# Rows of all batches as one stream of 14 tiles behind the attention, with a ring of three buffers for lifted products

## The reference

```python
def ffn(x, W1, b1, W2, b2):              # _quantize(W) = clip(round(W / (mean|W| + EPS)), -1, 1)
    h = relu(einsum('bsd,fd->bsf', x, _quantize(W1)) + b1)
    return einsum('bsf,df->bsd', h, _quantize(W2)) + b2
# xattn: layer norms with gains of both inputs, then softmax(q k^T * 32**-0.5) v, then @ Wo + bo
x = x + tanh(g_xattn[0]) * xattn(layernorm(x), ctx_1024, ...)
x = x + tanh(g_ffn[0]) * ffn(layernorm(x), ...)
```

## Time and profile before

| what | us |
|---|---|
| median of three runs | 971.6 (966.1 to 974.96) |
| the profiled execution, its own time | 969.31 |
| its span in the trace | 967.4 |
| PE busy | 902.7 (93%) |
| DVE busy | 734.4 (76%) |
| ACT busy | 644.1 (67%) |
| POOL busy | 303.1 (31%) |

### The profile page before, as it was taken

The page is one execution under the profiler, slowest core; times in us unless marked ns, Lnnn a source line. Parts: engine busy times, 40 slices in busy tenths (PEclk is TensorE's granted clock), DMA queues, the critical chain, the costliest instruction groups (busy, mean ns, idle before and its releaser), DMA issues.

```text
span 967.4 us, 22558 instructions
## 1 busy us (share of the span) xinstructions
PE 902.7 (93%) x8996; PEld 694.0 (72%) x8996; DVE 734.4 (76%) x1376; ACT 644.1 (67%) x1330; POOL 303.1 (31%) x519
## 2 busy tenths in 40 slices
PE   2998898899999999999999999999999999889768
PEld 0555566666798688867888688967887688668747
...
GB/s 270 139 228 222 180 110 195 165 135 1 8 138 153 24 2 92 101 127 1 32 113 175 2 2 105 109 106 1 43 102 90 2 2 144 62 29 2 24 19 20
DMA packets 52104, 84.02 MB, mean 87 GB/s; under 512 B 6520, under 2 KB 33592, under 8 KB 51000
## 3 DMA queue, kind: packets, MB, share of 16 engines
...
q10 hardware_dynamic: 432, 0.02, 0.0%
...
## 4 chain that ended last, share of the span: by engine, by line
PE 78%; DVE 9%; DMA 5%; SPq 3%; ACT 3%; issue 1%; POOL 1%; DVEq 0%; ACTq 0%; POOLq 0%
PE ps_fill L477 49%; PE ps_pv L524 8%; PE ps_score L492 7%; PE ps_exp L508 7%; PE ps_fill L534 4%; DMA ctx_raw<-ctx_in 2%; DVE row_max L785 2%; SPq L398 2%; DVE p_parts L793 2%; PE ps_fill L583 2%; DMA h_parts<-w2t 2%; DMA k_stack<-k_stage_lo 1%; SPq L407 1%; DVE ctx_t_lo L870 1%; DVE bn L825 1%
## 5 line engine op out<-in xcount | busy, mean ns | idle before, releaser
L793 DVE TENSOR_TENSOR p_parts<-ps_exp,p_parts 125x448 f16<-125x448 f32 x384 | 231.4, 617 | 61.5 <-ACT ps_exp L664 59.5
L785 DVE TENSOR_REDUCE row_max<-ps_score 128x1 f32<-128x750 f32 x256 | 238.7, 933 | 47.4 <-PE ps_score L492 46.6
L663 ACT ACTIVATE p_parts<-ps_exp 125x448 f16<-125x448 f32 x384 | 209.1, 544 | 94.6 <-PE ps_exp L508 81.0
L664 ACT ACTIVATE ps_exp<-ps_exp 125x448 f32<-125x448 f32 x384 | 211.2, 550 | 0.0
L492 PE MATMUL ps_score<-k_stack,q_stack 96*128 96x375 f16 x512 | 126.7, 329 | 13.2 <-DVE row_max L785 12.2
L508 PE MATMUL ps_exp<-q_stack,k_stack 99*125 99x224 f16 x768 | 128.0, 266 | 9.3 <-DVE p_parts L793 6.3
L524 PE MATMUL ps_pv<-v_now,p_parts 125*128 125x66 f16 x3072 | 115.3, 194 | 2.4 <-DVE p_parts L793 1.9
L477 PE MATMUL ps_fill<-w_ternary,h_parts 128*128 128x256 fp8e4 x1024 | 116.6, 273 | 0.0
L524 PEld LDWEIGHTS ps_pv<-v_now,p_parts 125*128 125x128 f16 x3072 | 110.0, 98 | 8.3 <-DVE p_parts L793 2.1
L508 PEld LDWEIGHTS ps_exp<-q_stack,k_stack 99*125 99x125 f16 x768 | 88.0, 138 | 33.8 <-DVE p_parts L793 9.3
L477 PEld LDWEIGHTS ps_fill<-w_ternary,h_parts 128*128 128x128 f16 x1024 | 99.7, 98 | 13.2 <-DVE ctx_t_lo L870 1.2
...
## 6 DMA issues: line engine op xcount, KB each, us to landing
...
```

The costliest lines, as they stand in the source:

```text
L663: nc.scalar.activation(ph[0:KR, unit, :], ps_exp[0:KR, u, 0:2 * NQ], ACT.Exp, scale=EXP_SCALE)
L664: nc.scalar.activation(ps_exp[0:KR, u, 0:2 * NQ], ps_exp[0:KR, u, 0:2 * NQ], ACT.Exp, scale=EXP_SCALE).then_inc(exp_done, 1)
L785: nc.vector.tensor_reduce(mx[:, i // 2, i % 2:i % 2 + 1], ps_score[:, :, 0:KH], AX.XY, ALU.max) \
L793: nc.vector.tensor_tensor(pl[0:KR, unit, :], ps_exp[0:KR, u, 0:2 * NQ], ph[0:KR, unit, :], ALU.subtract).then_inc(p_split, 1)
```

## The change

Four things are changed together.

1. **A stream of 14 tiles.** Behind the attention the 8 x 224 rows are one stream of 1792 rows. Batch n handles the tiles that are complete with it: 1, 2, 2, 2, 1, 2, 2, 2 for n = 0 to 7. `o_t` holds two halves of 256 columns, and `ot` may write a piece in each. `op`, `norm2`, `yt`, `f2`, `store` follow `tiles_of(n)`; `f1` streams 256 columns in a batch of two tiles and 128 in a batch of one.
2. **`mr` in two matmuls.** The maxima of a pair of heads are 4 stationary columns, and ACT writes the four rows into both heads; a mask in four rows of `k_stack` (`minus_m`, made with `pick`) takes the right two. The shift is added to the maxima by `split`.
3. **A ring of three.** `lifted` has three buffers for `q`, `k` and `f1` in place of two and two. A lift waits until POOL has made the low part of the lift three before it (`parted`).
4. **Another order.** OPENING, ROUND and ENDING are written anew. Small tiles are put into memory that is free at the time, and constants are set in another way.

```diff
+TILES = B * NQ // P
-SPLIT_ROWS = 3 * HD
-MAX_END = SPLIT_ROWS + 2
-STACK_ROWS = MAX_END + 1
+STACK_ROWS = SPLIT_ROWS + 4
...
+def tiles_before(n):
+    return n * NQ // P
+def tiles_of(n):
+    return tiles_before(n + 1) - tiles_before(n)
+LIFTS = [s for s in STEPS if s[0] in ("q", "k", "f1")]
+LIFT_AT = {s: k for k, s in enumerate(LIFTS)}
...
-        qk_full = sb("qk_full", [P, 2, 2 * NQ], F32)
-        h_full = sb("h_full", [P, 2, 2 * NQ], F32)
-        o_t = [sb(f"o_t_{part}", [P, DC, NQ], F16) for part in ("hi", "lo")]
+        lifted = sb("lifted", [P, 3, 4 * P], F32)
+        o_t = [sb(f"o_t_{part}", [P, 2, DC, 2 * P], F16) for part in ("hi", "lo")]
...
+        PARTED = {"q": (qk_split, 10, 0), "k": (qk_split, 10, 2), "f1": (h_split, 8, 0)}
+        def parted(kind, i, n):
+            s, per_batch, first = PARTED[kind]
+            return s, n * per_batch + (first + i + 1)
+        def o_pieces(t, n):
+            at, end = n * NQ - tiles_before(n) * P, tiles_before(n + 1) * P - n * NQ
+            frm, to = q_cols(t)
+            cut = min(max(end, to.start), to.stop)
+            found = [(to.start, cut, n % 2, at), (cut, to.stop, (n + 1) % 2, -end)]
+            return [(slice(a - QSTART[t], b - QSTART[t]), half, slice(a + add, b + add))
+                    for a, b, half, add in found if b > a]
...
                 elif kind == "mr":
                     pe.wait_ge(max_split, n * 8 + (i + 1))
-                    for h in (2 * i, 2 * i + 1):
-                        for t in range(2):
-                            frm, to = q_cols(t)
-                            last = pe.matmul(
-                                ps_fill[SPLIT_ROWS:MAX_END, bank, (h % 2) * NQ + to.start:(h % 2) * NQ + to.stop],
-                                mhl[:, h, t, :], ident16[:, frm], start=True, stop=True,
-                                tile_position=(0, SPLIT_ROWS))
+                    for t in range(2):
+                        frm, to = q_cols(t)
+                        last = pe.matmul(ps_fill[SPLIT_ROWS:STACK_ROWS, bank, to], mhl[:, t, 2 * i:2 * i + 2, :],
+                                         ident16[:, frm], start=True, stop=True, tile_position=(0, SPLIT_ROWS))
...
                 elif kind == "f1":
+                    wide = tiles_of(n) * P
                     for j in range(2):
                         m = slice((2 * i + j) * P, (2 * i + j + 1) * P)
-                        last = three(ps_fill[:, bank, j * NQ:(j + 1) * NQ], lambda a, c: w1q[:, c, m],
-                                     lambda a, c: o_t[a][:, c, :], order=((0, 0), (0, 1)))
+                        last = three(ps_fill[:, bank, j * wide:(j + 1) * wide], lambda a, c: w1q[:, c, m],
+                                     lambda a, c: o_t[a][:, n % 2, c, 0:wide], order=((0, 0), (0, 1)))
...
                 act.wait_ge(fill_ready, ready)
+                if kind in ("q", "k", "f1"):
+                    lift = LIFT_AT[kind, i, n]
+                    if lift >= 3:
+                        act.wait_ge(*parted(*LIFTS[lift - 3]))
```

More of the change, by code:

```diff
@@ L65 @@
[L65 to L79, removed]
@@ L100 @@
-    part.14@1 part.15@1 max.20@1 pv.5@1 stat.6@3 expo.20@1 yt.1@0 part.16@1 expo.21@1 max.21@1 k.7@2 stat.7@3
-    score.23@1 f1.0@0 norm.6@3 part.17@1 score.24@1 take.4@1 part.18@1 f1.1@0 expo.22@1 score.25@1 f1.2@0 yt_lo.0@0
-    expo.23@1 score.26@1 v.3@2 pv.6@1 v_lo.2@2 take.5@1 expo.24@1 expo.25@1 max.22@1 vc.2@1 part.19@1 rstd.0@3
-    yt_lo.1@0 part.20@1 score.27@1 norm.0@3 max.23@1 v.4@2 score.28@1 max.24@1 expo.26@1 mr.5@1 pv.7@1 k_hi.6@2
-    expo.27@1 f1.3@0 f1.4@0 split.5@1 f1_hi.0@0 max.25@1 max.26@1 pv.8@1 expo.28@1 reload.13@0 mr.6@1 part.21@1
@@ new lines @@
+    ternary.13@0 score.12@1 part.3@1 max.10@1 yt_lo.1@0 expo.8@1 part.4@1 ot_lo.0@0 max.11@1 k.3@2 part.5@1
+    split.2@1 take.0@1 max.12@1 k_hi.1@2 part.6@1 ot_lo.1@0 pv.1@1 score.13@1 expo.9@1 op.0@0 expo.10@1 mr.2@1
+    score.14@1 k.4@2 score.15@1 v.0@2 expo.11@1 expo.12@1 pv.2@1 part.7@1 expo.13@1 part.8@1 max.13@1 ternary.14@0
+    stat.0@3 op_add.0@0 max.14@1 k_hi.2@2 rstd2.0@0 score.16@1 stat.1@3 stat.2@3 v.1@2 score.17@1 mr.3@1 reload.10@0
+    kq.2@1 expo.14@1 vc.1@1 reload.11@0 reload.12@0 kq.3@1 norm2.0@0 max.15@1 pv.3@1 part.9@1 expo.15@1 split.3@1
@@ new lines @@
+    f1.1@0 score.25@1 k.7@2 norm.1@3 expo.25@1 norm.2@3 max.19@1 norm.3@3 score.26@1 v.4@2 score.27@1 norm.6@3
+    f1.2@0 max.20@1 v_lo.2@2 k_hi.5@2 pv.7@1 expo.26@1 stat.7@3 rstd.0@3 score.28@1 part.18@1 mr.5@1 f1.3@0
+    expo.27@1 score.29@1 max.21@1 f1.4@0 k_hi.6@2 max.22@1 take.5@1 part.19@1 part.20@1 part.21@1 max.23@1 expo.28@1
+    pv.8@1 mr.6@1 v_lo.3@2 max.24@1 expo.29@1 score.30@1 norm.4@3 max.25@1 expo.30@1 part.22@1 f1_hi.0@0 max.26@1
+    v.5@2 f1_hi.1@0 part.23@1 split.5@1 k_hi.7@2 split.6@1 take.6@1 part.24@1 max.27@1 cx.0@3 v_lo.4@2 part.25@1
@@ L131 @@
-    f1.0@-1 part.17@0 norm.0@2 score.24@0 stat.6@2 rstd.0@2 mr.4@0 part.18@0 expo.22@0 pv.6@0 expo.23@0 f1.1@-1
-    score.25@0 max.21@0 take.4@0 expo.24@0 yt_lo.0@-1 f1.2@-1 part.19@0 expo.25@0 f1.3@-1 pv.7@0 v_lo.2@1 stat.7@2
-    mr.5@0 score.26@0 expo.26@0 max.22@0 norm.1@2 f1.4@-1 ctx.0@2 yt_lo.1@-1 score.27@0 norm.6@2 max.23@0 part.20@0
-    v.3@1 store.0@-2 k_hi.6@1 expo.27@0 take.5@0 expo.28@0 max.24@0 part.21@0 expo.29@0 norm.2@2 v.4@1 score.28@0
-    expo.30@0 pv.8@0 f1.5@-1 part.22@0 vc.3@0 v.5@1 f1_hi.0@-1 expo.31@0 score.29@0 expo.32@0 f1_hi.1@-1 split.5@0
@@ L170 @@
-    op.1@7 yt.0@7 yt.1@7 f1.0@7 ot_lo.1@7 op_add.0@7 bias.0@7 f1.1@7 f1.2@7 f1.3@7 op_add.1@7 f1.4@7 rstd2.0@7
-    yt_lo.0@7 yt_lo.1@7 xb.0@7 f1_hi.0@7 f1.5@7 f1_hi.1@7 f1_hi.2@7 store.0@7 f1.6@7 f1_hi.3@7 f1.7@7 f2.0@7
-    f1_hi.4@7 f2.1@7 f1_hi.5@7 f2.2@7 f1_hi.6@7 f1_hi.7@7 f2.3@7 f2_add.0@7 f2_add.1@7 f2_add.2@7 f2_add.3@7
-    bias2.0@7
+    split.0@7 vc.2@7 kq.3@7 part.44@6 split.1@7 take.13@6 mr.1@7 expo.0@7 score.8@7 store.0@5 xb.0@6 f2_add.3@5
+    vc.3@7 max.7@7 pv.15@6 expo.1@7 part.45@6 part.46@6 take.14@6 part.47@6 store.0@6 max.8@7 expo.2@7 take.15@6
```

430 lines of the change are left out of this document (224 added, 206 removed).

## The result

The changed kernel took 958.1 us (median of 6 runs, 956.0 to 959.9) and the kernel before 972.6 us beside it: ratio 0.9855, 95% interval 0.9829 to 0.9882, or 14.5 us less. I had forecast 24 us less, 947.6 us. The time lies inside my range (936 to 962), near its upper end.

A forecast was written before the change was run, and what follows sets the result against it. PE was taken to bound the rounds, without a gap. PE work -26.6, give-backs +3, +5 and +0.6, and order -6 sum to -24.0 us: 969.3 becomes 945.3, plus 2.3 for the median 947.6 us; range 936 to 962.

The forecast's parts named there:

- R3: Rival for batches 0 and 4: narrow `f1` matmuls are paced by weight loads, 96 ns each, +10, 957.6 us; chance 0.08.
- half is the nearer end: `mr` on PE: two matmuls for four nearly halve its cost, -0.145 us for each of 64 groups, -9.3 us.
- a give-back of 5: From 105 to 286.7 us, batch 0: DVE becomes the bound and takes back +5 us of PE's gain.
- DVE the pace from 105 to 190 us: Stretch of the kernel before: DVE is the fullest engine, 78.8 of 85 us, and at 93% was the pace.
- give-back 6.1 instead of 3: Round with batch 4's rows: about 91 us of PE, DVE about 82, 90% full, takes back +3 us (0 to 8).
- the 91 to 97 that I had named as a sign: Sign: the round with batch 4's rows would take 91 to 97 us.
- I take -6, half of the idle time: Ending: the new order moves about 12 us of PE work ahead into full rounds, -6 us, bounds +10 and -14.
- in the rounds it can win nothing, since PE has no gap: Rounds: the new order gains no time there and only moves work ahead, so no gain was counted.
- +2.4: Tail: +1.8 us for eight wide `f1` and +0.6 because they begin at the low clock.
- R1: Rival on the lifts: the ring of three stalls ACT behind k's low parts, 59 us over seven batches, 1007 us; chance 0.07.
- R2: Rival for batches 0 and 4: DVE and the score-maximum loop keep their pace, no gain, 971.6 or 965 us; chance 0.11.
- R4: Rival: the order is better than allowed, start and ending give 11 us more, 936 us; chance 0.13.

The follow-up runs named there:

- the old order: Changed kernel with OPENING, ROUND and ENDING of the kernel before, two and two lift buffers, feed-forward bias left out: 973.2 us, ratio 1.0008.
- 11.6 us less work on it: Changed kernel with each row maximum on DVE reading only 375 of its 750 scores: 945.3 us, ratio 0.9732 to the kernel before.
- the shifted `f2`: Changed kernel with batch 4's `f2.1` moved to where `f2.3` stands, plus 44 unread matmuls behind the last `op` of batch 7: 953.6 us, ratio 0.9791.
- the ring of four: Changed kernel with four buffers for lifted products instead of three, feed-forward bias left out: 955.8 us, ratio 0.9824 to the kernel before.
- the ending with narrower `f1`: Changed kernel with `f1` streaming 224 columns instead of 256 in batches of two tiles: 949.6 us, ratio 0.9777 to the kernel before.
- the two repeats: Changed kernel measured again without an edit in two other groups: 958.3 us (0.9842) and 956.9 us (0.9831).

## Why the prediction was right and where it was wrong

**The counts and prices of PE work: right, but for `mr`.** `f2` stayed at 3.50 us and wide `f1` came to 1.75. The timeline of the changed kernel around a narrow `f1` (start, duration) has 16 matmuls whose starts are 56 ns apart:

```profile
662.83 0.22 PE L519 MATMUL ps_fill<-o_t_hi,w_ternary 128*128 128x128 f16 x1
662.89 0.22 PE L519 MATMUL ps_fill<-o_t_lo,w_ternary 128*128 128x128 f16 x1
...
663.67 0.22 PE L519 MATMUL ps_fill<-o_t_lo,w_ternary 128*128 128x128 f16 x1
```

So R3 is refuted. The Trainium skill gives about 81 ns for 128 columns ("TensorE: Matmul & The Clock Gate", Back-to-back issue gap). The trace doesn't agree: this stream has 56. The term "half is the nearer end" of `mr` was mis-sized: 0.075 a group by the rounds and 0.10 by the chain, for 0.145. By the rounds this is 0.56 us in a full round, which is the 0.5 by which it outgrew my sum (+1.13 for +0.6).

**Batch 0: near in size, by luck.** I had -11.3 with a give-back of 5; the profile shows -11.6, and the eight profiles with this opening -12 to -18. But the old order keeps only 3.8 of it: the new order does its work here, where I gave it none. My give-back was too small for the old order, and the gain of the new one covered it. I had also called DVE the pace from 105 to 190 us. In the view of the chain over that stretch of the kernel before, the transfers `h_parts<-w2t` and `k_stack<-k_stage_lo` and SP's waits at L398 and L407 make 35% (12.4, 9.7, 9.6, 3.6), and the maxima and `p_parts` on DVE 18%.

**The round with batch 4's rows: give-back 6.1 instead of 3, still within my 0 to 8, and for another reason.** Its 97.3 us lie just over the 91 to 97 that I had named as a sign. I argued from a DVE 90% full. DVE was 84% busy, and with 11.6 us less work on it the round gave 0.6. PE's waits are 3.7 us, of 0.4 to 1.6 each, at the same four places in all three profiles of the changed kernel. The two longest (2.9 us) are those of `expo.42` and `expo.46`, where the order gives PE an `f2` that a batch of one tile doesn't have. Of the rest of the give-back 0.6 is the price of `mr`; for the other 2 us no wait shows. The chain of the changed kernel there, from the difference before to the held `expo.46`:

```profile
707.04 0.53 DVE p_parts L838
707.57 0.66 DVE ctx_t L915
708.24 0.84 DVE row_max L830
709.08 0.54 DVE p_parts L838
709.62 0.04 issue
709.67 0.41 PE ps_exp L550 x2
```

PE waits for DVE's sequence and not for its total: the shifted `f2` made one wait go and another come.

**The step that failed: "I take -6, half of the idle time", for the new order in the ending.** Instead of 81.4 - 4.2 the ending took 87.0. The new order did move `score`, `expo` and `pv` ahead, but the new ENDING as a whole gave nothing: with the old one the changed kernel took 956.4 us for 958.3. PE's waits of the changed kernel in the ending (818 to 905 us), the four largest:

```profile
PE ps_score L534 <- DVE row_max L830: 7.6, 9, 1.1
PE ps_fill L624 <- POOL row_max_parts L1120: 1.8, 3, 1.0
PE ps_pv L566 <- DVE p_parts L838: 1.5, 1, 1.5
PE ps_exp L550 <- DVE p_parts L838: 1.0, 3, 0.5
```

Waits for the maxima were 5.2 us in the kernel before. The view of the chain from 818.4 to 905.4 passes through all engines: four lines of PE make 61% of it, the maxima 10.5%. That the loop of `score`, maximum and split paces it is my reading; of 8.8 us less for DVE in it only 2.6 to 3.0 came back.

Three things bear on the 5.6 us. Some 2.5 go with the order of the ending. Some go with the clock: it is at 1.2 GHz for 6.8 us (the window of 841.7 in the first fence: 42 matmuls, 5.6 us busy), and for 0.8 us in the kernel before (0.99 over its ending). In the 3.7 us before this fall PE was busy 2.55. The profiles with the new ENDING and whole `f1` and maxima line up by it: with 3.4 us at the low clock 86.4 (the ring of four), with 6.8 us 87.1 to 87.2 (four profiles), with 10.2 us 87.7. That is 0.6 us for 3.4, so I estimate 1.1 of the 5.6 us from it. By the same estimate the ending with narrower `f1` (13.6 us at the low clock) would be 88.3 with the wide one, and was 87.9: 0.4 for 1.8 us of PE work. The remaining 2 us stay open, and so does what sets the clock off: no experiment changed it alone, and in batch 4's round it fell in three of seven profiles behind the same waits.

**The new order elsewhere: missed.** It is worth 15.0 us and not 6, and they come from OPENING and ROUND: before the third `expo` and in batch 4's round. The new ENDING wins some 3.5 us in the tail and loses 2.5 ahead of it, which the medians don't tell from nothing. My sentence "in the rounds it can win nothing, since PE has no gap" was read from the kernel before. The gaps came with the removed work.

**The tail: the term right in size, the stage not.** I had +2.4, and it stayed at 50.9 (51.8 and 50.7 in the two repeats). The 256 matmuls took 30.46 for 28.60, +1.9 as wider `f1` wants. But the 24 matmuls of `op` took less than before, as the clock was granted, and I had no term for that. The chains over them, of the kernel before, of the changed one, and of the one with the old order:

```profile
919.77 6.68 PE ps_fill L477 x24
```

```profile
908.03 5.35 PE ps_fill L519 x24
```

```profile
919.33 8.05 PE ps_fill L525 x24
```

**The rivals.** R1 (the ring) is refuted by the ring of four. R2, no gain from the narrow batches, has the number that the old order gives (971.6 for 973.2), but not its mechanism: there both batches give 9.3 us (3.8 and 5.5), and the other stages take 12.6. I held it for a property of the batches; it is one of the order. R3 has the measured time to half a microsecond, 957.6 for 958.1, and its mechanism is refuted: the number alone would have misled. R4 was wrong on the ending. That 958.1 lies in my range is owed to the width of the range. The forecast itself was 10.5 us off, and its errors partly cancel: 9.8 us too hopeful in the ending and 3.1 in batch 4's round, against 2.4 too cautious in the tail.
